# Cross-attention and bit-weight FFN on one core: more softmax tiles turned by DMA, their values last in TensorE's step

## The chip, the cores and the metric

One NeuronCore of a Trainium2 chip runs the whole program. The time is the device time of that core in microseconds; of the runs of a kernel the median is taken.

## The reference

The input is x (4, 1024, 1024), the context ctx (4, 1024, 1024), and the weights of a linear layer that are given as four sigmoid "bits" per weight. All is float32.

```python
x = x + attention(layernorm(x), ctx, ctx)       # 16 heads of 64, causal, softmax over keys, scale 1/8
weight = einsum('oin,n->oi', sigmoid(pweight) - sigmoid(nweight), exps * sigmoid(mask)) * scale
bias   = round(|clip(einsum('on,n->o', pbias - nbias, bexps), -1, 1)| * 15) / 15 * sign * biasscale
x = x + einsum('bsi,oi->bso', layernorm(x), weight) + bias
```

Keys and values are both the context as it stands; there are no projections.

## The kernel before

**Work.** The 4 x 1024 query rows are 32 tiles of 128 rows, t = 0..31, eight per batch; i = t % 8 is the place in the batch, and a tile sees i + 1 blocks of 128 keys. A tile is cut into jobs: four heads each for i = 0 and 1 (4 jobs), two for i = 2 and 3 (8 jobs), one for i = 4 to 7 (16 jobs, the "long tiles"). q is a job's place in its tile, n its number over the whole program (352 jobs), and a job has `blocks` = heads x (i + 1) blocks of probabilities, each 128x128. Products are made to near float32 accuracy by splitting an operand into a high and a low float16 part: scores take two matmuls, values three.

**A job's life.** PE (TensorE) makes the scores in PSUM (`slot`, two places, L397 to L421). DVE (VectorE) takes the row maxima (L642). ACT (ScalarE) makes the exponentials p in SBUF (`p32`, two places, L537) and their row sums. Then p must be turned, so that the keys lie on the partitions. In the usual way PE transposes the blocks into PSUM (`ptb`, two banks, L429), in chunks of at most four blocks; ACT writes the high parts into `pt` (L553), DVE the low parts (L648). Some jobs are "turned" by DMA instead (`j.d` is their count, L57): ACT scales and rounds p into the high part right after its exponentials (L546), DVE writes the low part beside it from SBUF (L656), both in `p16`, and the SP queue issues one DMA transpose of both parts into `ptd` (L320). PE then multiplies the turned probabilities by the values (L449, L450, L452) into `obank`, four heads to a group. When a group's last job is in, DVE's `output` divides by the row sums (L662, L667) and sets `obank` free, and POOL (GpSimd) adds the result to the row of x in `ring` (L870).

**The order.** Nothing is scheduled by a program; each engine's list is written out by hand as a loop over the jobs, and semaphores tie the engines. "Step j" of an engine is the turn of that loop for job j:

- PE: scores(j+2), values(j-2), transposes(j), then a share of the FFN's matmuls for tile t-3 (L468, 48 per tile).
- ACT: high parts of j (this first waits until values(j-2) are done, L550, also when j has none), exponentials(j+2) with the copy L546 if j+2 is turned, and at some steps the high part of a context, q or y tile.
- DVE: maxima(j+2), the low part L656 if j+1 is turned, output of the group that j-2 closed, low parts of j, then at some steps statistics for a layer norm (L674, L677) or a half of the FFN's result (L709).
- POOL: the add of a closed group (L870), at step 2 of a long tile the low part of y (L856), at 6 that of the context (L851), at 9 the bias (L864), at 11 the low part of q (L845); at 5 and at the end of a tile it normalises a row (L828).
- SP: the DMAs; in step s the transposition of job s + 1, loads of x and the context at step 9, the transposes of context, q and y (16 blocks each), the store of a result.

Of a long tile, jobs q = 3, 6, 9, 12, 15 are turned before, and of a tile of two heads (t > 3) jobs 3 and 6: 92 jobs. `p16` and `ptd` are the two halves of the tensor `pd`, which holds weights at the start.

## Time and profile before

| | |
|---|---|
| runs of the kernel before, median of 3 | 1187.38 us (1184.31 to 1188.52) |
| the profiled execution | 1185.72 us |
| its span, first to last instruction | 1183.9 us |
| TensorE clock granted, mean of the span | 0.990 |
| busy: PE / DVE / ACT / POOL | 1098.5 / 994.4 / 862.3 / 492.7 us |

The profile follows one execution. "Busy" is time in which an engine has an instruction under way; matmuls are pipelined and their ends modelled, so PE's share reads high. DVE and ACT start an instruction some 0.1 us before the one ahead has drained, so the durations of neighbours overlap. A timeline row gives start, duration, engine, line, operation and tile; in brackets stands the idle time of the engine ahead of it and what ended it.

### The profile page before, as it was taken

How to read it: one execution, taken by the hardware profiler on the slowest of the kernel's cores; microseconds unless marked ns; L12 is line 12 of the kernel's file. 1: busy time of each engine (PE TensorE's matmuls, PEld its weight loads, DVE VectorE, ACT ScalarE, POOL GpSimd, SP SyncE). 2: the span in 40 equal slices, each digit the busy share in tenths (PEclk: the TensorE clock that was granted, in tenths of full speed). 3: DMA queues.
4: the chain of work that ended last, by engine and by line, in shares of the span. 5: the costliest groups of instructions: out<-in, count | busy, mean ns of one | idle time of the engine just before them, and what ended most of it. 6: DMA issues, size and time to landing. Idle time of an engine off the chain costs nothing.

```text
span 1183.9 us, 32049 instructions
## 1 busy us (share of the span) xinstructions
PE 1098.5 (93%) x13092; PEld 808.7 (68%) x13092; DVE 994.4 (84%) x1552; ACT 862.3 (73%) x1770; POOL 492.7 (42%) x510
## 2 busy tenths in 40 slices
PE   3778888999999999999999999999999999999988
PEld 3666665666766777777776777777776676777753
DVE  5765688899988988998988888999988888998962
ACT  5887865777786777778776777777786777877740
POOL 3343534433334754344235654343335655331150
PEclk9999999999999999999999999999999999999999
DMA  8999936577659877775678887667768976654443
GB/s 308 301 295 337 299 80 120 134 146 122 151 121 186 189 180 131 162 160 112 132 121 203 194 173 148 139 140 130 137 125 205 185 171 131 137 117 86 89 90 71
DMA packets 382594, 191.13 MB, mean 161 GB/s; under 512 B 358128, under 2 KB 358128, under 8 KB 378352
## 3 DMA queue, kind: packets, MB, share of 16 engines
q1 hardware_dynamic: 381440, 189.05, 70.4%
q8 instruction: 104, 1.70, 0.6%
q14 instruction: 42, 0.34, 0.1%
q10 hardware_dynamic: 1008, 0.04, 0.1%
HBM read 67.15 MB, written 16.78 MB: 71 GB/s over the span
## 4 chain that ended last, share of the span: by engine, by line
PE 47%; DVE 18%; ACT 14%; DMA 7%; issue 7%; SPq 4%; POOL 3%; ACTq 0%; POOLq 0%; DVEq 0%
PE ffnb L468 15%; PE ptb L429 8%; PE slot L415 5%; PE slot L416 5%; DVE pd L656 4%; ACT p L537 4%; DVE mx L642 4%; DMA pd<-pd 4%; ACT pd L546 4%; PE obank L449 4%; ACT pt L553 4%; PE obank L452 3%; DVE stats L674 3%; PE obank L450 3%; DVE pt L648 3%
## 5 line engine op out<-in xcount | busy, mean ns | idle before, releaser
L537 ACT ACTIVATE p<-slot,mx 128x512 f32<-128x512 f32 (+7 forms) x512 | 377.4, 745 | 135.1 <-issue 71.2
L642 DVE TENSOR_REDUCE mx<-slot 128x1 f32<-128x640 f32 (+7 forms) x352 | 356.0, 1014 | 32.0 <-PE slot L419 31.3
L468 PE MATMUL ffnb<-wt,yt 128*128 128x512 f16 x1464 | 372.1, 380 | 1.1 <-DMA yt<-y 0.8
L648 DVE SCALAR_TENSOR_TENSOR pt<-ptb,pt 128x512 f16<-128x512 f32 (+1 forms) x504 | 281.6, 598 | 51.8 <-ACT pt L553 50.3
L553 ACT ACTIVATE pt<-ptb 128x512 f16<-128x512 f32 (+1 forms) x504 | 239.9, 526 | 106.0 <-PE ptb L429 104.8
L415 PE MATMUL slot<-kt,qt 128*128 128x128 f16 (+3 forms) x1056 | 267.2, 283 | 14.0 <-ACT p L537 5.9
L416 PE MATMUL slot<-kt,qs 128*128 128x128 f16 (+3 forms) x1056 | 267.2, 283 | 0.0
L870 POOL TENSOR_TENSOR ring<-ring,att 128x256 f32<-128x256 f32 x128 | 94.2, 736 | 394.0 <-DVE att L667 393.9
L429 PE MATMUL ptb<-id,p 128*128 128x128 f32 x1700 | 238.3, 279 | 10.9 <-DVE pt L648 10.8
L468 PEld LDWEIGHTS ffnb<-wt,yt 128*128 128x128 f16 x1464 | 137.2, 98 | 100.1 <-issue 2.2
L449 PE MATMUL obank<-v,pt 128*128 128x64 f16 x1700 | 176.9, 193 | 16.3 <-DVE att L667 12.1
L429 PEld LDWEIGHTS ptb<-id,p 128*128 128x128 f32 x1700 | 181.9, 141 | 13.9 <-issue 12.3
L449 PEld LDWEIGHTS obank<-v,pt 128*128 128x128 f16 x1700 | 153.5, 98 | 35.6 <-DVE att L667 20.1
L450 PE MATMUL obank<-v,pt 128*128 128x64 f16 x1700 | 176.7, 193 | 0.0
L452 PE MATMUL obank<-v,pt 128*128 128x64 f16 x1700 | 176.7, 193 | 0.0
L415 PEld LDWEIGHTS slot<-kt,qt 128*128 128x128 f16 x1056 | 103.4, 98 | 79.5 <-ACT p L537 11.7
L452 PEld LDWEIGHTS obank<-v,pt 128*128 128x128 f16 x1700 | 151.8, 98 | 0.0
L450 PEld LDWEIGHTS obank<-v,pt 128*128 128x128 f16 x1700 | 151.6, 98 | 0.1
L416 PEld LDWEIGHTS slot<-kt,qs 128*128 128x128 f16 x1056 | 103.6, 98 | 56.4
L656 DVE SCALAR_TENSOR_TENSOR pd<-p,pd 128x640 f16<-128x640 f32 (+3 forms) x92 | 111.8, 1215 | 13.5 <-ACT pd L546 10.5
L419 PE MATMUL slot<-maskb,idb 128*128 128x128 bf16 x512 | 110.3, 220 | 0.0
L537 ACT ACTIVATION_READ_ACCUMULATOR p<-slot,mx 128x1 f32 x512 | 106.4, 208 | 0.0
(92 smaller groups left out, 1528.7 us busy)
## 6 DMA issues: line engine op xcount, KB each, us to landing
ring<-in_x_dram SPq DMA_DIRECT2D x32, 512.0 KB, 4.5
cin<-in_ctx_dram SPq DMA_DIRECT2D x32, 512.0 KB, 4.9
out_dram<-ring SPq DMA_DIRECT2D x32, 512.0 KB, 3.3
qs<-qt SPq DMA_DIRECT2D x124, 128.0 KB, 2.9
v<-in_weights_dram SPq DMA_DIRECT2D x11, 1024.0 KB, 8.1
kt<-in_weights_dram SPq DMA_DIRECT2D x11, 1024.0 KB, 8.0
pd<-in_weights_dram SPq DMA_DIRECT2D x5, 1024.0 KB, 7.3
yt<-in_weights_dram SPq DMA_DIRECT2D x5, 1024.0 KB, 10.0
```

The lines of the kernel that those rows point to most:

```text
L415: pe.matmul(dst, qt[:, t % 2, h, :], keys, start=True, stop=False, skip_group_check=True)
L416: last = pe.matmul(dst, qs[:, h, :], keys, start=False, stop=end <= i, skip_group_check=True)
L429: last = pe.transpose(ptb[:, c % 2, at * P:(at + 1) * P], p32[:, j.par, k * P:(k + 1) * P], id32[:, :])
L449: pe.matmul(dst, turned[:, k, :], v[:, 0:D], start=blk == 0, stop=False, skip_group_check=True)
L450: pe.matmul(dst, turned[:, k, :], v[:, D:2 * D], start=False, stop=False, skip_group_check=True)
L452: last = pe.matmul(dst, turned[:, j.blocks + k, :], v[:, 0:D], start=False, stop=blk == j.i, skip_group_check=True)
L468: last = pe.matmul(dst, yt[:, k % 2, a * KT_N + kk, :], wt[:, c, kk, half * 512:half * 512 + 512], start=r == 0, stop=r == 3 * KT_N - 1)
L537: last = nc.scalar.activation(p32[:, j.par, hh * j.keys:(hh + 1) * j.keys], slot[:, j.par, base:base + j.keys], ACT.Exp, bias=mx[:, j.par, ...
L553: nc.scalar.activation(pt[:, j.par, blocks.start:blocks.stop, :], ptb[:, c % 2, 0:P * len(blocks)].rearrange("p (k c) -> p k c", c=P), ACT ...
L642: nc.vector.tensor_reduce(mx[:, j.par, 0:j.heads], src[:, 0:j.heads, 0:j.keys], AX_X, ALU.max, negate=True).then_inc(mx_ready, 1)
L648: nc.vector.scalar_tensor_tensor(pt[:, j.par, j.blocks + blocks.start:j.blocks + blocks.stop, :], ptb[:, c % 2, 0:P * len(blocks)].rearran ...
L656: nc.vector.scalar_tensor_tensor(p16[:, size:2 * size], p32[:, j.par, 0:size], P_SCALE, p16[:, 0:size], ALU.mult, ALU.subtract).then_inc(p ...
```

## The change

It changes which jobs are turned by DMA: in a long tile each odd q (8 of 16 instead of 5), in a tile of two heads q = 3, 5, 7 (3 of 8 instead of 2), 146 jobs in all. They have two places each for the split (`p16`) and for the turned form (`ptd`): `pd` grows to three parts, two for `p16`; the second place of `ptd` is `pt[:, 1]`, which the usual way used for odd jobs. The semaphore of the landing is doubled with them, and the waits follow the places. PE does the values of a turned job as the last thing of step j + 2, after the FFN's matmuls, no longer right after the scores; DVE's output of a group that a turned job closed goes from the middle of the step to its end. In a long tile every group is closed by a turned job.

```diff
--- before.py
+++ after.py
@@ -54,7 +54,7 @@
         self.blocks = blocks = self.heads * (self.i + 1)
 
 
-        self.d = turned if self.heads < 3 and t > 3 and q > 0 and q % 3 == 0 else None
+        self.d = turned if self.heads < 3 and t > 3 and q % 2 and q >= self.heads * 2 - 1 else None
         count = -(-blocks // 4) if self.d is None else 0
         size = -(-blocks // count) if count else 0
         self.chunks = [(chunk0 + c, range(size * c, min(size * c + size, blocks))) for c in range(count)]
@@ -70,6 +70,13 @@
         JOBS.append(Job(len(JOBS), _t, _q, sum(len(j.chunks) for j in JOBS), sum(j.d is not None for j in JOBS)))
 FIRST.append(len(JOBS))
 TURNED = [j for j in JOBS if j.d is not None]
+
+def used_before(j):
+
+    earlier = [k.n for k in JOBS[:j.n] if (k.d % 2 == j.d % 2 if k.d is not None else j.d % 2 and k.par)]
+    return earlier[-1] + 1 if earlier else 0
+
+
 LAST_OF_GROUP = [j.n for j in JOBS if j.closes_group]
 
 
@@ -187,7 +194,7 @@
         v16 = sb("v16", [P, V_PLACES, H, 2 * D], F16)
         kt16 = sb("kt16", [P, K_PLACES, H, P], F16)
         ring = sb("ring", [P, RING, DM], F32)
-        pd = sb("pd", [P, 2, 2 * 8 * P], F16)
+        pd = sb("pd", [P, 3, 2 * 8 * P], F16)
         cin = sb("cin", [P, DM], F32)
         norm32 = sb("norm32", [P, DM], F32)
         q16 = sb("q16", [P, H, 2 * D], F16)
@@ -215,8 +222,8 @@
         bvec = sb("bvec", [P, 8], F32)
 
 
-        p16 = pd[:, 0]
-        ptd = pd[:, 1].rearrange("p (k c) -> p k c", c=P)
+        p16 = [pd[:, 0], pd[:, 1]]
+        ptd = [pd[:, 2].rearrange("p (k c) -> p k c", c=P), pt[:, 1]]
 
 
         def chunk_place(places):
@@ -226,7 +233,7 @@
                  chunk_place(kt16[:, 7:9].rearrange("p a h c -> p (a h c)")),
                  chunk_place(kt16[:, 5:7].rearrange("p a h c -> p (a h c)")),
                  chunk_place(v16[:, 6:8].rearrange("p a h c -> p (a h c)")),
-                 chunk_place(pd[:, :, :].rearrange("p a c -> p (a c)")),
+                 chunk_place(pd[:, 0:2, :].rearrange("p a c -> p (a c)")),
                  chunk_place(yt[:, :, :, :].rearrange("p a k c -> p (a k c)"))]
         coef_diag = ring[:, 6, 0:NBITS * P].rearrange("p (n q) -> p n q", n=NBITS)
 
@@ -265,7 +272,8 @@
 
         s_done, mx_ready, p_done = sem("s_done"), sem("mx_ready"), sem("p_done")
         t_done, hi_done, lo_done, pv_done = sem("t_done"), sem("hi_done"), sem("lo_done"), sem("pv_done")
-        p16_hi, p16_lo, pt_in = sem("p16_hi"), sem("p16_lo"), sem("pt_in")
+        p16_hi, p16_lo = sem("p16_hi"), sem("p16_lo")
+        pt_in = [sem(f"pt_in{r}") for r in range(2)]
         osb_done = sem("osb_done")
         rinv_ready, x1_ready = sem("rinv_ready"), sem("x1_ready")
         q_stats, q_mv, q_rs, q_norm, q_hi, q_lo = (sem("q_" + n) for n in ("stats", "mv", "rs", "norm", "hi", "lo"))
@@ -315,9 +323,9 @@
 
             def turn_p(j):
                 sp.wait_ge(p16_lo, j.d + 1)
-                if j.d > 0:
-                    sp.wait_ge(pv_done, TURNED[j.d - 1].n + 1)
-                sp.dma_start_transpose(ptd[:, 0:2 * j.blocks], p16[:, 0:2 * P * j.blocks]).then_inc(pt_in, 16)
+                reached(sp, pv_done, used_before(j))
+                sp.dma_start_transpose(ptd[j.d % 2][:, 0:2 * j.blocks], p16[j.d % 2][:, 0:2 * P * j.blocks]
+                                       ).then_inc(pt_in[j.d % 2], 16)
 
             def swap_q(t, half):
                 heads = slice(H // 2 * half, H // 2 * (half + 1))
@@ -438,8 +446,8 @@
                 if j.d is None:
                     pe.wait_ge(lo_done, j.chunks[-1][0] + 1)
                 else:
-                    pe.wait_ge(pt_in, 16 * (j.d + 1))
-                turned = pt[:, j.par] if j.d is None else ptd
+                    pe.wait_ge(pt_in[j.d % 2], 16 * (j.d // 2 + 1))
+                turned = pt[:, j.par] if j.d is None else ptd[j.d % 2]
                 for hh in range(j.heads):
                     h = j.head0 + hh
                     for blk in range(j.i + 1):
@@ -510,7 +518,7 @@
             for j in JOBS:
                 if j.n + 2 < len(JOBS):
                     scores(JOBS[j.n + 2])
-                if j.n > 1:
+                if j.n > 1 and JOBS[j.n - 2].d is None:
                     values(JOBS[j.n - 2])
                 transpose_p(j)
                 if j.n < UNITS:
@@ -519,6 +527,8 @@
                     bias_part(j.n - BIAS_JOBS[0])
                 for k, m0, m1 in matmuls_at(j.t, j.q):
                     linear(k, m0, m1)
+                if j.n > 1 and JOBS[j.n - 2].d is not None:
+                    values(JOBS[j.n - 2])
             values(JOBS[-2])
             values(JOBS[-1])
             pe.wait_ge(p_done, len(JOBS))
@@ -541,9 +551,9 @@
                 last.then_inc(p_done, 1)
                 if j.d is not None:
                     act.wait_ge(p_done, j.n + 1)
-                    reached(act, pt_in, 16 * j.d)
+                    reached(act, pt_in[j.d % 2], 16 * (j.d // 2))
                     size = P * j.blocks
-                    nc.scalar.activation(p16[:, 0:size], p32[:, j.par, 0:size], ACT.Copy, scale=P_SCALE
+                    nc.scalar.activation(p16[j.d % 2][:, 0:size], p32[:, j.par, 0:size], ACT.Copy, scale=P_SCALE
                                          ).then_inc(p16_hi, 1)
 
             def high_parts(j):
@@ -653,8 +663,9 @@
             def low_part_unturned(j):
                 dve.wait_ge(p16_hi, j.d + 1)
                 size = P * j.blocks
-                nc.vector.scalar_tensor_tensor(p16[:, size:2 * size], p32[:, j.par, 0:size], P_SCALE,
-                                               p16[:, 0:size], ALU.mult, ALU.subtract).then_inc(p16_lo, 1)
+                split = p16[j.d % 2]
+                nc.vector.scalar_tensor_tensor(split[:, size:2 * size], p32[:, j.par, 0:size], P_SCALE,
+                                               split[:, 0:size], ALU.mult, ALU.subtract).then_inc(p16_lo, 1)
 
             def output(g):
                 dve.wait_ge(p_done, LAST_OF_GROUP[g] + 1)
@@ -777,8 +788,9 @@
                     maxima(JOBS[j.n + 2])
                 if j.n + 1 < len(JOBS) and JOBS[j.n + 1].d is not None:
                     low_part_unturned(JOBS[j.n + 1])
-                if j.n > 1 and JOBS[j.n - 2].closes_group:
-                    output(JOBS[j.n - 2].group)
+                ended = JOBS[j.n - 2] if j.n > 1 and JOBS[j.n - 2].closes_group else None
+                if ended is not None and ended.d is None:
+                    output(ended.group)
                 low_parts(j)
                 if j.n + 1 < UNITS:
                     first_difference(j.n + 1)
@@ -801,6 +813,8 @@
                             result(k, half)
                 for k in y_begun(t, s):
                     y_moments(k)
+                if ended is not None and ended.d is not None:
+                    output(ended.group)
             output(GROUPS * TILES - 1)
             spare = slot[:, 0, 0:512]
             for k in range(TAIL, TILES):
```

In the compiled order DVE's list shows what a turned job meets. The rows are of a tile of eight key blocks (i = 7); `mx<-slot` are maxima, `pd<-p,pd` the low part of a turned job, `pt<-ptb,pt` low parts of one that PE transposes. Before:

```order
L656 SCALAR_TENSOR_TENSOR pd<-p,pd 128x1024
L648 SCALAR_TENSOR_TENSOR pt<-ptb,pt 128x512 x2
L642 TENSOR_REDUCE mx<-slot 128x1
L674 BN_STATS stats<-ring 128x6 x2
L677 BN_AGGR mv<-stats 128x2
L642 TENSOR_REDUCE mx<-slot 128x1
L648 SCALAR_TENSOR_TENSOR pt<-ptb,pt 128x512 x2
L642 TENSOR_REDUCE mx<-slot 128x1
L656 SCALAR_TENSOR_TENSOR pd<-p,pd 128x1024
L662 RECIPROCAL rinv<-rowsum 128x4
L667 SCALAR_TENSOR_TENSOR att<-obank,rinv 128x256
```

And in the changed kernel, the same kind of tile:

```order
L678 SCALAR_TENSOR_TENSOR att<-obank,rinv 128x256
L652 TENSOR_REDUCE mx<-slot 128x1
L667 SCALAR_TENSOR_TENSOR pd<-p,pd 128x1024
L658 SCALAR_TENSOR_TENSOR pt<-ptb,pt 128x512 x2
L652 TENSOR_REDUCE mx<-slot 128x1
L685 BN_STATS stats<-ring 128x6 x2
L688 BN_AGGR mv<-stats 128x2
L652 TENSOR_REDUCE mx<-slot 128x1
L667 SCALAR_TENSOR_TENSOR pd<-p,pd 128x1024
L658 SCALAR_TENSOR_TENSOR pt<-ptb,pt 128x512 x2
L652 TENSOR_REDUCE mx<-slot 128x1
```

Between the maxima of a turned job and its low part stood two low parts `pt` and the next maxima; now the next maxima stand there alone, at some steps with an output or statistics. Of each two steps, one has the low parts of both kinds, the other none.

On PE, of a tile with five key blocks, `obank<-v,pd` are values of a turned job and `ffnb<-wt,yt` the FFN's matmuls. In the kernel before, the values stand right behind the scores:

```order
L415 MATMUL slot<-kt,qt 128x128
L416 MATMUL slot<-kt,qs 128x128
L419 MATMUL slot<-maskb,idb 128x128
L449 MATMUL obank<-v,pd 128x64
L450 MATMUL obank<-v,pd 128x64
L452 MATMUL obank<-v,pd 128x64
L449 MATMUL obank<-v,pd 128x64
```

In the changed kernel the FFN's matmuls come between:

```order
L424 MATMUL slot<-kt,qs 128x128
L427 MATMUL slot<-maskb,idb 128x128
L476 MATMUL ffnb<-wt,yt 128x512 x3
L457 MATMUL obank<-v,pd 128x64
L458 MATMUL obank<-v,pd 128x64
L460 MATMUL obank<-v,pd 128x64
L457 MATMUL obank<-v,pd 128x64
L458 MATMUL obank<-v,pd 128x64
```

## Rows read from the trace of the kernel before

**Rows 1.** The page, its first part: busy time of each engine.
```profile
PE 1098.5 (93%) x13092; PEld 808.7 (68%) x13092; DVE 994.4 (84%) x1552; ACT 862.3 (73%) x1770; POOL 492.7 (42%) x510
```
**Rows 2.** Windows on the four long tiles of the second batch; columns as the first line says.
```profile
core 0: us, PE busy (x) PEld busy (x) DVE busy (x) ACT busy (x) POOL busy (x), PEclk, DMA share, GB/s
444.60:483.60 39.00, 36.90 (x501) 27.39 (x497) 33.18 (x62) 27.45 (x63) 18.87 (x19) 1.00 0.73 146
...
567.40:614.30 46.90, 46.12 (x625) 34.23 (x624) 43.80 (x60) 37.43 (x63) 15.93 (x16) 1.00 0.73 135
sum 169.70, PE 163.73 PEld 122.21 DVE 153.46 ACT 129.89 POOL 66.84; mean PE 40.93 PEld 30.55 DVE 38.37 ACT 32.47 POOL 16.71
```
**Rows 3.** Timeline of DVE around a turned job, eight key blocks.
```profile
843.03 1.23 DVE L656 SCALAR_TENSOR_TENSOR pd<-p,pd 128x1024 f16<-128x1024 f32 x1 [0.25 <-ACT pd L546]
844.17 1.28 DVE L648 SCALAR_TENSOR_TENSOR pt<-ptb,pt 128x512 f16<-128x512 f32 x2
845.37 1.21 DVE L642 TENSOR_REDUCE mx<-slot 128x1 f32<-128x1024 f32 x1
846.50 1.27 DVE L674 BATCH_NORM_STATS2 stats<-ring 128x6 f32<-128x512 f32 x2
...
847.94 1.17 DVE L642 TENSOR_REDUCE mx<-slot 128x1 f32<-128x1024 f32 x1
```
**Rows 4.** Timeline of ACT in the same stretch.
```profile
840.70 1.12 ACT L537 ACTIVATE p<-slot,mx 128x1024 f32<-128x1024 f32 x1
...
841.94 1.06 ACT L546 ACTIVATE pd<-p 128x1024 f16<-128x1024 f32 x1
...
846.67 1.11 ACT L537 ACTIVATE p<-slot,mx 128x1024 f32<-128x1024 f32 x1 [1.60 <-issue]
```
**Rows 5.** Groups by line and shape: x count | busy us, mean ns | idle before.
```profile
L642 DVE TENSOR_REDUCE mx<-slot 128x1 f32<-128x1024 f32 x64 | 77.4, 1210 | 2.2 <-PE slot L419 1.9
L537 ACT ACTIVATE p<-slot,mx 128x1024 f32<-128x1024 f32 x64 | 71.5, 1117 | 30.5 <-issue 25.5 <-PE obank L452 3.6 <-DVE mx L642 1.2
L642 DVE TENSOR_REDUCE mx<-slot 128x1 f32<-128x640 f32 x64 | 51.4, 808 | 5.9 <-PE slot L419 5.9
L537 ACT ACTIVATE p<-slot,mx 128x640 f32<-128x640 f32 x64 | 51.0, 797 | 27.2 <-DVE mx L642 17.5 <-issue 7.3 <-PE obank L452 2.4
L546 ACT ACTIVATE pd<-p 128x640 f16<-128x640 f32 x20 | 14.7, 737 | 1.2 <-DMA pd<-pd 0.6
L648 DVE SCALAR_TENSOR_TENSOR pt<-ptb,pt 128x512 f16<-128x512 f32 x232 | 151.3, 683 | 28.3 <-ACT pt L553 27.6
L648 DVE SCALAR_TENSOR_TENSOR pt<-ptb,pt 128x384 f16<-128x384 f32 x228 | 119.3, 549 | 23.6 <-ACT pt L553 22.7
L648 DVE SCALAR_TENSOR_TENSOR pt<-ptb,pt 128x256 f16<-128x256 f32 x44 | 18.2, 413 | 0.0
```
**Rows 6.** The line L656 of DVE: duration ns shortest/median/longest, then the wait ahead of it.
```profile
L656 DVE SCALAR_TENSOR_TENSOR pd<-p,pd x92: 812/1092/2432, 194.9 to 1140.4; 128x768 f16<-128x768 f32 x26, 128x1024 f16<-128x1024 f32 x26, 128x640 f16<-128x640 f32 x20, 128x896 f16<-128x896 f32 x20
```
**Rows 7.** Timelines of DVE and POOL, six key blocks, where a group is closed.
```profile
773.46 0.94 DVE L642 TENSOR_REDUCE mx<-slot 128x1 f32<-128x768 f32 x1
...
778.82 2.14 DVE L656 SCALAR_TENSOR_TENSOR pd<-p,pd 128x768 f16<-128x768 f32 x1
...
775.02 0.73 POOL L870 TENSOR_TENSOR ring<-ring,att 128x256 f32<-128x256 f32 x1 [3.89 <-DVE att L667]
775.71 2.35 POOL L864 TENSOR_TENSOR ring<-ring,bias_row 128x1024 f32<-128x1024 f32 x1
778.02 2.13 POOL L845 TENSOR_TENSOR q<-norm,q 128x1024 f16<-128x1024 f32 x1
```
**Rows 8.** Timeline of PE's weight loads: the transposes of one job of six blocks.
```profile
921.54 0.64 PEld L429 LDWEIGHTS ptb<-id,p 128*128 128x128 f32 x6
```
**Rows 9.** SP's issue of the turned jobs' transposes (ns), and median us from issue to landing.
```profile
L320 SPq DMA_TRANSPOSE pd<-pd x92: 1274/1440/3463, 197.0 to 1141.7; - x92
...
pd<-pd SPq DMA_TRANSPOSE x92, 4.1
```

## The prediction

> **What bounds the kernel now.** I read the busy times first: PE 93% and DVE 84% of the span [rows 1]. Then windows, since such shares are means: in the four long tiles of a batch (169.7 us, and that four times in the 1184 of the span) PE is busy for 163.7, DVE for 153.5, ACT for 129.9 [rows 2]. With eight key blocks PE has work in 46.1 of 46.9 us and DVE in 43.8; with five, 36.9 and 33.2 of 39.0. So PE is the bound in the longest tiles, DVE stands 5 to 10% behind it, and whatever PE gives up, DVE soon takes over. The third view is the timeline around a turned job: ahead of its low part DVE has been idle for 0.25 us, until ACT's copy was done [rows 3]. DVE's filler (two low parts and one maxima) just about covers the way of a turned job through ACT. That is the place to watch, since the change takes the filler out.
>
> **PE.** There are 54 more turned jobs. Per batch the long tiles get three more each, of 5, 6, 7 and 8 blocks: 78 blocks, 312 in all. The two-head tiles with t > 3 get one more each, of 6 or 8 blocks, three times: 42. That makes 354 transposes fewer. Six take 0.64 us of weight loads [rows 8], 0.107 each, so PE sheds 37.9 us. Nothing else leaves PE; the values only move within a step.
>
> **ACT and DVE, by work alone.** With eight blocks an extra turned job takes two low parts of 0.68 from DVE [rows 5] and gives it one of 1.23 [rows 3]; with five it takes 0.55 + 0.41 and gives 0.81, the shortest of the line [rows 6]. DVE gains 0.13 to 0.15 a job, nothing that matters. DVE therefore still needs about 153 us of these tiles, where PE now needs 163.7 - 78 x 0.107 = 155.4.
>
> **The loop that the order makes.** In the changed order two steps hang together in a ring: maxima of turned job o, its exponentials (ACT), its copy (ACT), its low part (DVE), the low parts of job o - 1 (DVE, behind it in DVE's list), then the maxima of o + 2. Between the maxima of o and its low part DVE has only the maxima of o + 1. Eight blocks, link by link: maxima 1.21; 0.09 to the exponentials (846.58 to 846.67) [rows 3, 4], the longer gap of a job whose forerunner by two was turned, which now is every turned job; exponentials 1.12 [rows 5]; 0.12 to the copy, copy 1.06, 0.03 to DVE (843.00 to 843.03) [rows 3, 4]; low part 1.14 from start to start, low parts of o - 1 1.20 from start to start [rows 3]. Sum **5.97 us for two steps**, 47.8 for the tile, against 46.9 measured. Five blocks: 0.81 + 0.09 + 0.80 + 0.12 + 0.74 + 0.03 + 0.74 + 0.80 [rows 5, 6], neighbours on DVE overlapping by 0.08 (846.58 to 846.50) [rows 3], = 4.13, 33.0 for the tile, against 39.0. Six and seven lie evenly between, 4.74 and 5.36. The four tiles take 161.6 us by the ring. It is longer than PE's 155.4 and DVE's 153, so neither engine is the bound: their hand-over is.
>
> **What comes on top on DVE.** In the ring DVE is idle between the maxima of o + 1 and the low part of o. The way there is 2.42 us with eight blocks and 1.78 with five, the maxima fill 1.13 and 0.73: 1.29 and 1.05 idle. Outputs fit in. At step 3 stand the statistics of q, 1.44 from start to start of what follows (846.50 to 847.94) [rows 3], too long by 0.15 to 0.39. At step 15 half a result (512 columns from PSUM like a chunk of low parts, 0.60) and the statistics of y, 2.04, too long by 0.75 to 0.99. Over the four sizes: 4.6 us a batch.
>
> **What comes on top from POOL.** One low part of a turned job in the trace took 2.14 us, and it ended 0.81 us after POOL's low part of q (778.02 + 2.13 = 780.15, then 780.96) [rows 7]; the lone duration for six blocks lies between the 0.81 of five and the 1.23 of eight, near 0.95. It stood still for all but 0.15 us of the overlap. I take it that of DVE's work here only this line is stopped: it alone reads two tensors in SBUF, the others read PSUM or one tensor. Where do the new low parts meet POOL? The output of a group comes at the end of steps 1, 5, 9 and 13, right behind maxima. From the end of those maxima to POOL's add it is 0.62 us (774.40 to 775.02), the add lasts 0.69, and behind it stands at step 9 the bias, 2.35 [rows 7], at step 1 the low part of y, same shapes as that of q, 2.13. POOL is so busy until 3.66 and 3.44 us after the maxima; the low part of q = 11 and of q = 3 is due after 1.78 to 2.42. It is late by 1.24 to 1.88 and 1.02 to 1.66, less the 0.15: 1.09 to 1.73 and 0.87 to 1.51. Over four sizes 5.6 and 4.8, together **10.4 us a batch**. Before, job 3 had a step's low parts more ahead of it and job 11 wasn't turned; job 12 met the low part of q, and the measured 169.7 holds that already.
> The Trainium skill, page SBUF — State Buffer, section "SBUF: two separate sides", says that VectorE and GpSimd share a pair of ports by an exclusive lock: an op with two SBUF inputs against a GpSimd op that reads SBUF "fully blocks" for the whole instruction. Without the 0.15 us of grace each stall would be longer by that, 1.2 us a batch, 5 us in all; the row of 2.14 us speaks for the shorter figure, and the rule speaks for the stall as such and against this change.
>
> **Other edits.** The doubled places let the transposition of job o start without waiting for the values of the turned job before; before, the issue came after it anyway, so I cost that at nothing, bounds 0 and -2 us. Values last: with the ring as the bound PE idles some 0.5 us a pair of steps at eight blocks (46.1 - 24 x 0.107 = 43.5, an eighth is 5.44, against 5.97), which covers it; were PE late, the exponentials of o + 2 (they wait for values(o - 2), and the high parts stand behind them) and the next group's first values (behind DVE's output) would be next. SP has 54 more issues of 1.44 us [rows 9] with nothing urgent behind. DMA: a turned job lands 4.1 us after issue [rows 9]. Its values must be done before ACT begins the exponentials of the job four later: low parts, a whole ring, maxima and gap after its own low part, 0.80 + 4.13 + 0.90 = 5.8 us with five blocks, 1.20 + 5.97 + 1.30 = 8.5 with eight. That leaves 1.7 us for the values at five blocks, with DMA engines that are 73% busy already [rows 2]: the cover is thin only there. Cost 0, bounds 0 and +20 us. Two-head tiles: 42 transposes of the 354, 4.5 us; I take half, 2.2, with bounds 0 and 4.5, since DVE does the low parts of y, context and q there.
>
> **Sum.** By batch 161.6 + 4.6 + 10.4 = 176.6 against 169.7: +6.9. By size: five blocks 33.0 + 1.4 + 3.2 = 37.6 (39.0 before, so faster), eight blocks 47.8 + 0.9 + 2.0 = 50.7 (46.9 before, slower by 8%). Four batches: +27.6, less 2.2: +25.4. The profiled execution took 1185.7, so 1211; the median shown is 1.7 above it, and the three casts a tile on ACT, which I haven't priced, can only delay the exponentials: **1214 us**.
>
> **Rivals.**
> *PE's gain comes through.* If the copy comes early enough that DVE never waits for it, PE stays the bound: 1187 - 38 = **1149**. For it: PE's 98% of the longest tile. Against it: DVE already waits with two low parts more as filler [rows 3], and DVE's own work needs 153 of 155. It decides if the way from maxima to low part is under 1.2 us at eight blocks; the links add up to 2.42. Chance 0.10.
> *The ring holds, POOL slips by.* If POOL's work starts later than I place it, in the stretch of the next maxima, the 10.4 us go: 166.2 a batch, -3.5 x 4 - 2.2 = -16, **1171**. This is the other side by one mechanism, at steps 2 and 10, decided by whether POOL's work begins over 1.2 us later than in rows 7. Against it: the add waits for DVE's output alone. Chance 0.13.
> *The DMA becomes late.* 146 transposes in place of 92, with the engines at 73%. If landings stretch from 4.1 to over 6 us, five and six blocks pay about 1 us a job, 64 jobs: +20 to +30 on top, **1240**. Chance 0.09.
>
> **Chances.** My forecast has 0.68, with a range of its own of 1195 to 1232. A measurement tells about 0.3% from no change. Slower by more: 0.68 + 0.09 less a little for the low edge, 0.75; faster by more: 0.10 + 0.13 less a little, 0.20; within, 0.05. The range leaves out PE's gain (0.10) and the far end of the late DMA: 1165 to 1243.
>
> **What would show it.** The waits: DVE's low part of a turned job waits for ACT's copy at nearly each of the 146 (0.25 us where it shows before, 0.9 to 1.3 us now), some 60 to 120 us in all, the largest wait of DVE. The same line's longest durations fall on q = 3 and q = 11, near 2.5 us and more at five blocks. PE's busy time falls by some 38 us while the span grows. Windows: tiles of five blocks shorter, of eight blocks near 50 us. I am wrong if DVE's idle time ahead of that line stays under 30 us, if the eight-block tiles take 46 us or less, or if PE waits long for the landing.

## The result, and the profile after

The changed kernel takes **1246.28 us** (median of 4 runs, 1242.72 to 1248.6); the kernel before took 1187.95 in the same series (4 runs, 1184.31 to 1188.95). The ratio is 1.0499, 95% interval 1.0474 to 1.0525: slower by 58 us, where 27 were forecast. It lies 14 us above the forecast's own range (1195 to 1232) and 3 us above the wide one (1165 to 1243). The direction was right, the size was not.

The page of the changed kernel, busy time of each engine, against [rows 1]:

```profile
PE 1086.3 (88%) x12738; PEld 775.4 (62%) x12738; DVE 1024.0 (83%) x1498; ACT 860.2 (69%) x1716; POOL 529.0 (43%) x510
```

PE's share fell from 93% to 88%, DVE's hardly moved: no engine is the bound. Weight loads fell by 33 us of the 38 forecast, PE's modelled busy time by 12 only; part of the gap is the clock (last section). Waits of the changed kernel (engine, line, what it waited for: us in total, times, longest), and of the kernel before, a choice of rows:

```profile
PEld obank L457 <- DVE att L678: 94.5, 72, 4.0
...
DVE pd L667 <- ACT pd L556: 76.9, 103, 1.9
PE obank L457 <- DVE att L678: 76.5, 70, 3.9
ACT p L547 <- PE obank L460: 70.2, 52, 3.1
...
ACT pt L563 <- PE obank L460: 16.3, 6, 3.7
```

```profile
PEld obank L449 <- DVE att L667: 20.9, 32, 1.5
...
ACT p L537 <- PE obank L452: 13.2, 14, 1.3
PE obank L449 <- DVE att L667: 12.5, 28, 1.2
...
DVE pd L656 <- ACT pd L546: 10.5, 32, 0.9
```

Two kinds of wait have grown. The one that the prediction named, DVE's low part behind ACT's copy, is 76.9 us in 103 times (of 146 turned jobs, where "nearly each" was forecast; in the pairs that begin with jobs 1 and 5 DVE's own list fills the gap). The other it named only to put it at nothing: PE's values wait for DVE's output (76.5 against 12.5), and ACT for PE's values, partly at its high parts (16.3 us in 6 times, up to 3.7 at once; before, no such row).

Where the time lies: windows of the long tiles of the second batch (columns as in [rows 2]), then of the short tiles behind them, after and before.

```profile
454.80:497.20 42.40, 37.59 (x485) 26.41 (x485) 35.82 (x57) 28.19 (x61) 19.84 (x18) 0.96 0.87 178
497.20:538.40 41.20, 37.03 (x484) 26.58 (x483) 36.74 (x57) 30.48 (x59) 17.61 (x16) 1.00 0.86 166
538.40:583.90 45.50, 40.70 (x540) 29.02 (x539) 40.81 (x57) 33.84 (x59) 18.36 (x16) 1.00 0.79 161
583.90:633.30 49.40, 44.19 (x600) 31.34 (x600) 44.49 (x57) 37.16 (x59) 19.02 (x16) 1.00 0.84 157
```
```profile
633.30:650.60 17.30, 16.04 (x191) 11.76 (x190) 10.82 (x19) 10.51 (x36) 2.93 (x5) 0.90 0.85 179
650.60:671.90 21.30, 18.75 (x172) 12.71 (x173) 20.64 (x34) 15.27 (x48) 13.65 (x16) 1.00 0.83 173
671.90:700.80 28.90, 28.90 (x355) 21.26 (x352) 27.60 (x45) 20.08 (x50) 20.13 (x21) 1.00 0.96 172
700.80:734.50 33.70, 29.05 (x332) 21.35 (x329) 27.80 (x37) 21.50 (x47) 17.45 (x17) 0.95 0.72 147
```
```profile
614.30:629.90 15.60, 14.59 (x198) 10.73 (x199) 12.13 (x22) 11.55 (x41) 5.63 (x9) 1.00 0.84 162
629.90:648.40 18.50, 18.50 (x170) 12.47 (x167) 17.45 (x29) 13.41 (x41) 9.82 (x11) 1.00 0.83 194
648.40:678.00 29.60, 29.60 (x362) 21.98 (x359) 27.73 (x47) 21.25 (x53) 19.58 (x21) 1.00 0.82 192
678.00:706.00 28.00, 28.00 (x347) 21.60 (x343) 24.56 (x39) 21.56 (x48) 16.82 (x17) 1.00 0.81 165
```

The four long tiles take 178.5 us, against 169.7 before and 176.6 forecast. The tiles of i = 0, 1 and 3 (the first, second and fourth row of the second fence), where the change was costed at nothing or as a small gain, grew by 1.7, 2.8 and 5.7 us. The same by tile, as the mean over batches 2 to 4 (us; i = 7 without the last), for all kernels measured. A tile runs from the moment at which PE has the scores of its first job to the same moment of the next tile:

| i | before | after | a | b | e | f | c | d | lock | h | k | l |
|---|---|---|---|---|---|---|---|---|---|---|---|---|
| 0 | 15.7 | 17.2 | 17.2 | 17.3 | 15.7 | 16.8 | 16.8 | 17.4 | 17.1 | 15.8 | 15.8 | 15.8 |
| 1 | 18.6 | 21.0 | 18.7 | 18.6 | 21.7 | 20.9 | 20.6 | 21.4 | 19.8 | 18.6 | 18.8 | 18.6 |
| 2 | 29.5 | 28.8 | 28.8 | 28.9 | 29.5 | 30.2 | 28.8 | 28.8 | 28.8 | 28.9 | 28.8 | 28.8 |
| 3 | 28.0 | 33.7 | 27.1 | 29.0 | 29.7 | 29.6 | 33.0 | 33.6 | 33.1 | 27.1 | 27.1 | 27.1 |
| 4 | 39.2 | 42.6 | 40.6 | 42.6 | 44.3 | 40.2 | 42.8 | 42.5 | 38.1 | 39.5 | 40.7 | 39.7 |
| 5 | 40.0 | 41.2 | 41.8 | 41.2 | 44.3 | 41.3 | 40.3 | 41.1 | 38.8 | 40.2 | 41.0 | 40.8 |
| 6 | 44.0 | 45.5 | 45.5 | 45.5 | 49.2 | 45.3 | 43.5 | 45.1 | 43.3 | 43.7 | 45.7 | 46.0 |
| 7 | 47.4 | 49.4 | 49.5 | 49.5 | 51.9 | 49.5 | 47.3 | 49.4 | 47.3 | 47.1 | 50.9 | 49.9 |

A batch lost 17 us: 8 in the long tiles, 9 in the short ones. The letters are those of the experiments below (lock is i_lock).

**The ring.** DVE in the tile of eight blocks (start, duration, line, form; in brackets the idle time ahead and what ended it):

```profile
607.77 1.21 DVE L652 TENSOR_REDUCE mx<-slot 128x1 f32<-128x1024 f32 x1
...
609.10 0.42 DVE L678 SCALAR_TENSOR_TENSOR att<-obank,rinv 128x256 f32<-128x256 f32 x1
609.44 1.21 DVE L652 TENSOR_REDUCE mx<-slot 128x1 f32<-128x1024 f32 x1
611.39 1.23 DVE L667 SCALAR_TENSOR_TENSOR pd<-p,pd 128x1024 f16<-128x1024 f32 x1 [0.74 <-ACT pd L556]
612.53 1.28 DVE L658 SCALAR_TENSOR_TENSOR pt<-ptb,pt 128x512 f16<-128x512 f32 x2
613.73 1.21 DVE L652 TENSOR_REDUCE mx<-slot 128x1 f32<-128x1024 f32 x1
...
619.70 1.21 DVE L652 TENSOR_REDUCE mx<-slot 128x1 f32<-128x1024 f32 x1
...
623.32 2.33 DVE L667 SCALAR_TENSOR_TENSOR pd<-p,pd 128x1024 f16<-128x1024 f32 x1 [0.74 <-ACT pd L556]
...
626.78 2.34 DVE L652 TENSOR_REDUCE mx<-slot 128x1 f32<-128x1024 f32 x2
```

From the maxima of a turned job to those of the next it is 5.96 us (607.77 to 613.73), then 5.97, with the output inside the idle time: the ring as added up. With five to eight blocks the pairs without an extra (those that begin with jobs 7 and 13) take 4.12, 4.74, 5.35 and 5.97 us in nearly every tile, against 4.13, 4.74, 5.36 and 5.97 forecast. The last pair, of job 11, takes 7.08: its low part lasted 2.33. POOL at that time:

```profile
622.21 2.36 POOL L878 TENSOR_TENSOR ring<-ring,bias_row 128x1024 f32<-128x1024 f32 x1
624.53 3.12 POOL L859 TENSOR_TENSOR q<-norm,q 128x1024 f16<-128x1024 f32 x1
```

The bias ends at 624.57, the low part 1.08 later: it stood still for 1.10 us, forecast 1.09.

**What was not foreseen.** The seam between the long tiles and the next batch. At step 1 of the tile i = 0 the values of q = 15 of the tile before are due. PE, ACT and DVE there, in the changed kernel:

```profile
646.01 2.75 PE L476 MATMUL ffnb<-wt,yt 128*128 128x512 f16 x12
648.60 0.19 PE L457 MATMUL obank<-v,pt 128*128 128x64 f16 x1
...
653.15 0.20 PE L457 MATMUL obank<-v,pt 128*128 128x64 f16 x1 [2.59 <-DVE att L678]
649.50 0.60 ACT L563 ACTIVATE pt<-ptb 128x512 f16<-128x512 f32 x1 [3.74 <-PE obank L460]
650.13 0.69 DVE L658 SCALAR_TENSOR_TENSOR pt<-ptb,pt 128x512 f16<-128x512 f32 x1 [3.67 <-ACT pt L563]
652.67 0.42 DVE L678 SCALAR_TENSOR_TENSOR att<-obank,rinv 128x256 f32<-128x256 f32 x1
```

This step's own job is not turned, so ACT has high parts to write, and they wait for the values of j - 2. The transposes and twelve FFN matmuls now stand ahead of those values: ACT waits 3.74 us, DVE 3.67 behind it. DVE's output then comes last in its step, after y and a result, and PE, which must have it before the next group's first values, stands for 2.59 us. The six waits of ACT's high parts for values are all of this kind: three fall in tiles with i = 0, three in tiles with i = 3. Within a long tile there are none, since each step that ends with late values belongs to a turned job, which has no high parts. PE does wait for DVE's output inside the long tiles too (51.6 of the 76.5 us), but the late order isn't what makes the time there: with the old one (a_early, below) the tiles of six to eight blocks take 41.8, 45.5 and 49.5 us, no less than here.

### The profile page after: what moved, and what is told of

It reads as the page before. It is cut to its first block, busy times and chain, and to the rows that moved or that the text cites. A ratio compares the mean times of both kernels' runs of the same rounds, so it can differ in the third digit from the quotient of the medians.

```text
span 1240.9 us, 31340 instructions
## 1 busy us (share of the span) xinstructions
PE 1086.3 (88%) x12738; PEld 775.4 (62%) x12738; DVE 1024.0 (83%) x1498; ACT 860.2 (69%) x1716; POOL 529.0 (43%) x510
## 4 chain that ended last, share of the span: by engine, by line
PE 51%; DVE 17%; ACT 4%; issue 4%; DMA 4%; POOL 1%; SPq 1%; DVEq 0%; POOLq 0%; ACTq 0%
PE ffnb L476 19%; PE ptb L437 8%; PE slot L423 5%; PE slot L424 5%; DVE pd L667 5%; PE obank L457 4%; DVE pt L658 4%; DMA pt<-pd 4%; DVE mx L652 4%; PE obank L460 3%; PE obank L458 3%; ACT pd L556 2%; DVE att L678 2%; DVE stats L685 1%; PE slot L476 1%
## 5 line engine op out<-in xcount | busy, mean ns | idle before, releaser
L476 PE MATMUL ffnb<-wt,yt 128*128 128x512 f16 x1464 | 378.1, 385 | 1.7 <-DVE ring L720 0.9
L884 POOL TENSOR_TENSOR ring<-ring,att 128x256 f32<-128x256 f32 x128 | 100.2, 783 | 451.1 <-DVE att L678 451.1
L423 PE MATMUL slot<-kt,qt 128*128 128x128 f16 (+3 forms) x1056 | 269.0, 284 | 24.2 <-ACT p L547 20.6
L457 PE MATMUL obank<-v,pt 128*128 128x64 f16 x1828 | 193.0, 195 | 96.2 <-DVE att L678 76.5
L667 DVE SCALAR_TENSOR_TENSOR pd<-p,pd 128x768 f16<-128x768 f32 (+3 forms) x146 | 203.2, 1392 | 77.3 <-ACT pd L556 76.9
L563 ACT ACTIVATE pt<-ptb 128x512 f16<-128x512 f32 (+2 forms) x396 | 189.2, 526 | 95.9 <-PE ptb L437 79.2
L457 PEld LDWEIGHTS obank<-v,pt 128*128 128x128 f16 x1828 | 164.5, 98 | 138.5 <-DVE att L678 94.5
L658 DVE SCALAR_TENSOR_TENSOR pt<-ptb,pt 128x512 f16<-128x512 f32 (+2 forms) x396 | 222.7, 600 | 28.9 <-ACT pt L563 28.2
L437 PE MATMUL ptb<-id,p 128*128 128x128 f32 x1346 | 195.7, 286 | 1.1 <-DVE pt L658 1.1
L460 PE MATMUL obank<-v,pt 128*128 128x64 f16 x1828 | 192.3, 194 | 0.0
L458 PE MATMUL obank<-v,pt 128*128 128x64 f16 x1828 | 192.2, 194 | 0.0
L458 PEld LDWEIGHTS obank<-v,pt 128*128 128x128 f16 x1828 | 164.4, 99 | 6.8
L460 PEld LDWEIGHTS obank<-v,pt 128*128 128x128 f16 x1828 | 164.6, 99 | 0.0
L437 PEld LDWEIGHTS ptb<-id,p 128*128 128x128 f32 x1346 | 150.3, 145 | 1.6 <-issue 1.2
L556 ACT ACTIVATE pd<-p 128x768 f16<-128x768 f32 (+3 forms) x146 | 132.0, 904 | 4.6
```

What stands on the lines that cost most here:

```text
L423: pe.matmul(dst, qt[:, t % 2, h, :], keys, start=True, stop=False, skip_group_check=True)
L437: last = pe.transpose(ptb[:, c % 2, at * P:(at + 1) * P], p32[:, j.par, k * P:(k + 1) * P], id32[:, :])
L457: pe.matmul(dst, turned[:, k, :], v[:, 0:D], start=blk == 0, stop=False, skip_group_check=True)
L458: pe.matmul(dst, turned[:, k, :], v[:, D:2 * D], start=False, stop=False, skip_group_check=True)
L460: last = pe.matmul(dst, turned[:, j.blocks + k, :], v[:, 0:D], start=False, stop=blk == j.i, skip_group_check=True)
L476: last = pe.matmul(dst, yt[:, k % 2, a * KT_N + kk, :], wt[:, c, kk, half * 512:half * 512 + 512], start=r == 0, stop=r == 3 * KT_N - 1)
```

## The experiments

Ten kernels. a, b, e and f ask about the order, c about the ring, d and i about POOL, h, k and l which jobs to turn. Edits are shown against the changed kernel where nothing else is said.

**a_early: the change without its order.** Values and output of a turned job stand where the kernel before has them.

```diff
-                if j.n > 1 and JOBS[j.n - 2].d is None:
+                if j.n > 1:
                     values(JOBS[j.n - 2])
...
-                if j.n > 1 and JOBS[j.n - 2].d is not None:
-                    values(JOBS[j.n - 2])
...
-                if ended is not None and ended.d is None:
+                if ended is not None:
...
-                if ended is not None and ended.d is not None:
-                    output(ended.group)
```

> The changed kernel with one part undone: values of a turned job again right behind the scores, the output of its group again in the middle of DVE's step; the choice of jobs and the two places stay. Theory A (what my sum left out is the new order in steps whose own job is not turned: there the high parts on ACT wait for values that now come after transposes and the FFN's matmuls, and PE's next group waits for an output that stands behind statistics and results on DVE): the two-head tiles with eight blocks fall from 33.7 us back to about 28, the four-head tiles from 17 and 20-21 to under 16 and 19, the first long tile from 42.5 to about 39; the other long tiles stay at 41, 45.5 and 49. In all some 25 to 30 us less, 1217 to 1222. Rival B (the 54 more transposes crowd SP's queue and the DMA engines, and that makes the short tiles long): the short tiles stay where they are and PE waits more for landings, since values are wanted earlier: 1246 or more.

Measured: 1215.13 us (1213.21 to 1217.19), ratio to before 1.0237 (1.02 to 1.0273). The late order costs 31 us, more than half of the loss, and what is left is within 2 us of the forecast for the whole. By tile, i = 1, 3 and 4 give back 2.3, 6.6 and 2.0 us. Two points of the expectation didn't come: i = 0 stayed at 17.2 us, and i = 4 fell to 40.6, not to 39.

**b_both: late only where the step's own job is turned too.**

```diff
-                if j.n > 1 and JOBS[j.n - 2].d is None:
+                if j.n > 1 and (JOBS[j.n - 2].d is None or j.d is None):
                     values(JOBS[j.n - 2])
```

and the same condition at the three other places.

> The changed kernel with values last and the output at the end only in steps whose own job is turned too (that is inside long tiles and at steps 5 and 7 of two-head tiles), the old order in all other steps. Theory A: as much as undoing the order altogether, 1217 to 1222, apart from what steps 5 and 7 of the two-head tiles keep. Rival B: no change, within 5 us of 1246.

Measured: 1222.76 (1219.89 to 1227.86), 1.0305 (1.0262 to 1.0349). Most of the 31 us are the seams: 23 come back. Step 1 of the tiles i = 0 and i = 3 are such steps. The rest lies at i = 3 (29.0 against 27.1) and i = 4 (42.6 against 40.6); at step 1 of i = 4 the own job is turned, but DVE's output comes last all the same, behind a result and statistics. ACT's waits at the exponentials for PE's values stay in b_both (64.3 us) and so cost little.

**e_late: the kernel before with the late order alone.** Its 92 turned jobs and single places stay. The edit, against the kernel before:

```diff
-                if j.n > 1:
+                if j.n > 1 and JOBS[j.n - 2].d is None:
                     values(JOBS[j.n - 2])
...
+                if j.n > 1 and JOBS[j.n - 2].d is not None:
+                    values(JOBS[j.n - 2])
```

and DVE's output in the same way.

> The kernel before with one part of the change alone: its own 92 jobs, one place each, but values of a turned job last in PE's step and DVE's output of a group that it closed at the step's end. In this choice of jobs nearly every such step has a job of its own that PE transposes. Theory A (ACT's high parts wait for values that now stand behind transposes and FFN matmuls of the same step, and everything after them waits with them): each of the 92 late steps pays about 1 us, the values' delay of a job's transposes plus three FFN matmuls (0.53 + 0.64 at five blocks, 0.86 + 0.64 at eight) less the slack of some 0.5: 60 to 120 us more, 1245 to 1305, and ACT's wait for PE's values becomes its largest. Rival (the place of the values costs nothing by itself, what undoing it brought was the DMA's or SP's): within 10 us of 1187.

Measured: 1270.56 (1266.99 to 1273.31), 1.071 (1.069 to 1.073). With every third job turned, each late step belongs to a job that PE transposes, and has high parts waiting: the loss is 84 us, in the long tiles too (i = 6 49.2 against 44.0). Its waits show the mechanism by itself:

```profile
PEld obank L449 <- DVE att L669: 81.6, 59, 2.5
ACT pt L555 <- PE obank L452: 76.1, 71, 3.4
```

71 waits of ACT's high parts for values, none in the kernel before and 6 in the changed one: the same order is dear or nearly free, according to whose step it stands in.

**f_long: turned jobs in long tiles only,** the order late.

```diff
-        self.d = turned if self.heads < 3 and t > 3 and q % 2 and q >= self.heads * 2 - 1 else None
+        self.d = turned if self.heads < 2 and t > 3 and q % 2 and q >= self.heads * 2 - 1 else None
```

> The changed kernel with turned jobs in the long tiles only, none in the two-head tiles. Theory A: the eight-block two-head tile falls from 33.7 to 28 or 29 us and the four-head tiles that follow a long one keep their 17, since the last two turned jobs of a long tile still come late there; the first long tile falls from 42.5 to 39 or 40, the rest stays: some 25 us less, near 1221. A rival by which the long tiles' own DMA load makes the short ones slow would leave them at 33.

Measured: 1225.53 (1223.95 to 1229.32), 1.0338 (1.0317 to 1.036). The tile i = 1 keeps its 2.3 us though no job near it is turned but the q = 15 of the batch before: the seam of the rows above. i = 3 falls from 33.7 to 29.6, i = 4 from 42.6 to 40.2.

**c_short: the ring shortened.** ACT's copy is cut to 128 columns from tile 8 on (the high part beyond is left from an earlier job, and the low part takes the difference).

```diff
                     size = P * j.blocks
+                    size = size if j.t < 8 else P
```

> The changed kernel with ACT's copy of a turned job cut to its first 128 columns from the second batch on (tiles 8 to 31); the rest of the high part is left as it stands, so the low parts and values are those of other numbers. All waits stay. Theory R (the ring maxima, exponentials, copy, low part, low parts sets the pace of long tiles): the copy gives back 0.45 us a pair at five blocks and 0.75 at eight, up to PE's own pace of 5.44 a pair at eight: some 0.5 us x 8 pairs x 12 long tiles = 48 us less, near 1200. Rival P (PE or the DMA sets the pace and DVE's wait for the copy is slack): under 10 us.

Measured: 1227.53 (1222.92 to 1229.76), 1.0333 (1.0284 to 1.0381), 19 us less, not 48. The long tiles take 4.8 us a batch less, none of it with five blocks. DVE's wait for the copy fell from 76.9 to

```profile
DVE pd L668 <- ACT pd L557: 32.7, 52, 1.3
```

The cut shortens the copy of an eight-block job from 1.06 to 0.31 us, by 0.75, and where nothing else stands in a pair all of it arrives. In the tiles of eight blocks the pairs that begin with jobs 7 and 13 fall from 5.97 to 5.22 (610.33 to 615.55), and that of job 15 takes 5.22 too, where a_early has 5.97:

```profile
610.33 1.22 DVE L653 TENSOR_REDUCE mx<-slot 128x1 f32<-128x1024 f32 x1
...
615.55 1.22 DVE L653 TENSOR_REDUCE mx<-slot 128x1 f32<-128x1024 f32 x1
```

The other pairs hardly move, and the trace has a reason for each. In those of jobs 1 and 5 (6.58 and 5.98 us with either copy) DVE works through statistics or a result without a gap. In those of jobs 3 and 11 (6.87 and 7.08) the low part ends when POOL's operation does: it starts earlier and stands still longer (2.84 us instead of 2.34 at job 11). That of job 9 gains 0.24: in it DVE now waits for PE's scores (0.45 us). With five blocks job 13 gains 0.43 us and job 9 loses 0.75, because its low part now meets POOL (1.8 us instead of 0.9). So with eight blocks the ring alone sets the pace of three pairs in eight; my expectation gave the gain to all eight.

**d_bias: POOL's bias cut to one column** (the bias is left out of the rest).

```diff
-                nc.gpsimd.tensor_tensor(row, row, bias_row[:, :], ALU.add).then_inc(bias_added, 1)
+                nc.gpsimd.tensor_tensor(row[:, 0:1], row[:, 0:1], bias_row[:, 0:1], ALU.add).then_inc(bias_added, 1)
```

> The changed kernel with POOL's bias add cut to one column of 1024, so the bias is left out of all others; all waits stay. Theory L (DVE's low part of job 11 stands still while POOL adds the bias, and the ring passes that on): 1.1 us a long tile at eight blocks to 1.7 at five, 16 tiles, 22 us less, near 1224, and the low part of job 11 takes its lone length, 0.82 to 1.23. Rival (the stall falls into slack): under 5 us, while the low part of job 11 is as short.

Measured: 1239.78 (1237.99 to 1243.68), 1.0449 (1.0408 to 1.0489). The time alone doesn't tell the theories apart. POOL's list closed up, and the low part of q took the place of the bias:

```profile
809.41 0.20 POOL L878 TENSOR_TENSOR ring<-ring,bias_row 128x1 f32<-128x1 f32 x1
809.55 2.14 POOL L859 TENSOR_TENSOR q<-norm,q 128x1024 f16<-128x1024 f32 x1
```

DVE's low part of job 11 still took 2.2 to 2.5 us in the first three batches. The last two tiles of the program do tell: no low part of q follows there, job 11's low part took 1.09 and 1.23 us, and its pair 5.35 and 5.97, where the changed kernel has 6.68 and 7.09 in the same tiles. So the stall is POOL's, and the ring passes all of it on.

**i_lock: the three long POOL operations cut together** (bias as above; the low parts of q and y are written for one head and one block, the rest is left out).

```diff
-                nc.gpsimd.tensor_tensor(y16[:, 1, :, :], norm32[:, :].rearrange("p (k c) -> p k c", c=P),
-                                        y16[:, 0, :, :], ALU.subtract).then_inc(y_lo, 1)
+                nc.gpsimd.tensor_tensor(y16[:, 1, 0:1, :], norm32[:, 0:P].rearrange("p (k c) -> p k c", c=P),
+                                        y16[:, 0, 0:1, :], ALU.subtract).then_inc(y_lo, 1)
```

> The changed kernel with three of POOL's adds cut to a stub: the bias to one column, the low part of q to one head, the low part of y to one block; what is cut is left out of the result. The bias alone didn't tell, since the low part of q moved up into its place. Theory L: DVE's low part of jobs 3 and 11 takes its lone length (0.82 to 1.23, not 1.74 to 2.58), and the ring passes it on: 1.1 to 1.8 us at job 11 and 0.8 to 1.6 at job 3, 9.7 us a batch, 39 in all, near 1207; the tile of eight blocks 49.4 to 47.4, that of five blocks 42.5 to about 39.5. Rival (slack): under 10 us.

Measured: 1199.36 (1195.57 to 1201.92), 1.0109 (1.0089 to 1.0129), 47 us less than the changed kernel. The line L667 (count, shortest/median/longest ns) has no long ones of that kind left at jobs 3 and 11:

```profile
L667 DVE SCALAR_TENSOR_TENSOR pd<-p,pd x146: 815/1082/2042, 189.3 to 1153.5; 128x768 f16<-128x768 f32 x41, 128x1024 f16<-128x1024 f32 x41, 128x640 f16<-128x640 f32 x32, 128x896 f16<-128x896 f32 x32
```

there they take 0.82 to 1.23 us, and the pair of job 11 with eight blocks 5.96. The long tiles give back 11.2 us a batch, against 10.4 forecast. The pairs say where: those of job 11 give back 1.76, 1.54, 1.33 and 1.12 us with five to eight blocks, those of job 3 1.05, 0.80, 0.86 and 0.90. That is 9.4 of the 11.2, near the 9.7 expected. Nearly all of the rest is the first pair of the five-block tile (7.67 to 6.15); POOL's results also come earlier, and that part this run can't tell from the stalls.

**h_best: what the parts suggest.** The order of the kernel before, its choice in the long tiles (q = 3, 6, 9, 12, 15), but jobs 3, 5, 7 in two-head tiles; only job 5 uses the second place. Of the edit, the lines that choose jobs and places:

```diff
-        self.d = turned if self.heads < 3 and t > 3 and q % 2 and q >= self.heads * 2 - 1 else None
+        self.d = turned if self.heads < 3 and t > 3 and (q >= 3 and q % 2 if self.heads == 2 else q > 0 and q % 3 == 0) else None
+        self.place = 1 if self.heads == 2 and q == 5 else 0
```

> A version for use: the kernel before with its order and its choice in the long tiles (every third job), and of the change only the two-head tiles' jobs 3, 5 and 7, job 5 with the second place. Undoing the order showed these tiles at 27.1 and 28.8 us where the kernel before has 28.0 and 29.5, while the long tiles lose. Theory: 1.6 us less a batch in three batches, 5 us, 1181 to 1183 against 1187; the long tiles as before. Rival (the gain of the two-head tiles is given back at the seam to the first long tile, where its third turned job is still under way): no difference.

Measured: **1179.55 us** (1177.45 to 1183.07, 6 runs) against 1186.37 for the kernel before (11 runs): 0.9948 (0.993 to 0.9966). It is faster than both, by 0.5% against the kernel before, with an interval that leaves out 1. The tiles i = 2 and 3 take 28.9 and 27.1 us, against 29.5 and 28.0: 1.6 us a batch, 4.8 in the three batches that have such jobs. In the profiled executions h_best is 8 us shorter; most of the other 3 lie in the first three tiles and ahead of them, where no job is turned in either kernel, and why isn't known.

**k_shift5 and l_shift4: other jobs of the long tile.** On h_best, five or four turned jobs, away from POOL's low part of q.

```diff
-        self.d = turned if self.heads < 3 and t > 3 and (q >= 3 and q % 2 if self.heads == 2 else q > 0 and q % 3 == 0) else None
+        self.d = turned if self.heads < 3 and t > 3 and (q >= 3 and q % 2 if self.heads == 2 else q % 3 == 1) else None
```

(l_shift4: `q > 1 and q % 3 == 1`.)

> This is h_best (the order of the kernel before; in two-head tiles jobs 3, 5, 7 turned) with the five turned jobs of a long tile moved from q = 3, 6, 9, 12, 15 to q = 1, 4, 7, 10, 13. In h_best DVE's low part of q = 12 meets POOL's low part of q, and stalls 1.6 / 1.2 / 0.7 / 0.3 us with 5 / 6 / 7 / 8 key blocks; at the new places no low part of a turned job should lie beside a long operation of POOL, except near the start of a tile. Theory 'POOL's lock is worth what it stalls': 3.8 us a batch are freed, all of it at five and six blocks, where PE isn't the bound; over four batches up to 15 us, and with half of it lost to PE 1168 to 1176 us. Rival 'it comes back': job 1's low part and transposition meet the normalising on POOL and the queue of transposes at the start of a tile, and the time is 1178 to 1188 us.

> As k_shift5, without job 1: four turned jobs in a long tile, q = 4, 7, 10, 13. PE gets back 5 to 8 transposes a long tile, 0.107 us each, 11 us in all if PE is the bound throughout. Theory 'POOL's lock': if k_shift5 loses by its job 1, this one gains against it; the lock freed (up to 15 us) less PE's 11 us gives 1172 to 1182 us. Rival 'the fifth turned job is worth its 11 us and the lock is hidden': 1186 to 1192 us.

Measured: k 1211.22 (1210.04 to 1212.54), 1.0212 (1.0184 to 1.024); l 1202.04 (1199.99 to 1203.43), 1.0136 (1.011 to 1.0161). k missed both expectations by 23 us, l by 10. The premise failed too: the turned jobs didn't get away from POOL. At step 6 of a long tile POOL writes the low part of the context, and with seven and eight blocks the low part of job 7 meets it. In k_shift5:

```profile
607.55 2.82 DVE L668 SCALAR_TENSOR_TENSOR pd<-p,pd 128x1024 f16<-128x1024 f32 x1 [0.25 <-ACT pd L557]
607.15 2.13 POOL L864 TENSOR_TENSOR v<-cin,v 128x1024 f16<-128x1024 f32 x1
```

It took 2.97 and 2.82 us in three of the four batches, where 1.09 and 1.23 are its lone lengths. With what is left at five and six blocks, such a batch has 3.9 us of stalls or a little more, against 3.8 for job 12 in h_best: nothing was freed, so the two runs don't test whether freeing it pays. The loss lies in the long tiles, most with eight blocks (50.9 and 49.9 against 47.1). Where a group begins, PE waits for DVE's output of the group before, and the transposes of the step stand behind: 31.7 us in k_shift5, 13.2 in h_best, but 9.2 in l_shift4. ACT's exponentials wait for PE's values for 47.4 and 43.3 us in the two, against 7.3 in h_best. Which of these reach the end, and so what the 32 and 22 us are made of, wasn't tried.

## Why the prediction was right and wrong

**The loop that the order makes: right.** The four pair times came out within 0.02 us of the sum of links. DVE's wait for the copy, 60 to 120 us forecast as its largest, was 76.9. That the ring is the bound holds for pairs without an extra: with a copy shorter by 0.75 us those with eight blocks fell by 0.75 (c_short). In the others DVE's own list, POOL or PE's scores are as long.

**What comes on top from POOL: right.** Low parts of job 11 took 2.58, 2.40, 2.42 and 2.34 us for five to eight blocks, those of job 3 2.38, 1.74, 1.94 and 2.12; without POOL 0.82 to 1.23. Summed stalls: 5.6 us a batch for job 11, to the tenth as forecast, and 4.1 for job 3, where 4.8 were. The rule of the Trainium skill (page SBUF — State Buffer, section "SBUF: two separate sides"), that of two such operations the one that comes second "fully blocks", agrees but for the 0.15 us: 2.33 us ended 1.08 after the bias, when 1.23 would be a full restart.

**The step that failed: "Values last", under Other edits,** costed at nothing because the ring leaves PE idle. The cover argued for was PE's, in the middle of a long tile. I named who waits for the values ("the high parts stand behind them") and for the output ("the next group's first values"), and then didn't walk the list of steps in which values are late and high parts exist: step 1 of the tiles i = 0 and i = 3, behind a tile with turned jobs. Nor did I look at what else DVE has in a step whose output moves to its end. There nothing covers it. Measured price: 31 us (a_early), 23 of them where the step's own job isn't turned (b_both). That is the 32 us between forecast and result: 1214 was in effect the forecast of a_early, 1215.13. That these two agree to 1 us is in part luck. Without the late order five blocks took 3.0 us more than forecast, seven and eight 0.8 and 1.2 less, and the tile i = 0, put at nothing, 1.5 more a batch.

**What comes on top on DVE: half the size at one place, nearly right at the other.** Statistics of q: 1.1 us a batch forecast; the pairs of job 5 show 0.25, 0.17, 0.10 and 0.01 above the ring. Half a result and statistics of y: 0.75 to 0.99 a tile forecast; they show in the first pair of the next tile, which is 0.77, 0.70 and 0.61 above the ring with six to eight blocks.

**The long tiles as a whole:** 178.7 us a batch (mean) against 176.6, and 177.4 without the late order. The split by size was off. Eight blocks took 49.4 where 50.7 were forecast. Five took 42.6 where 37.6 were: its first pair is 7.5 to 7.8 us, where the ring alone gives 4.13 and a_early, which has the old order, 5.52. The tile also begins with the last low part of a two-head job, eight blocks wide, which stands still for POOL (1.89 us at 456.77); the sum had no term for this seam. So "tiles of five blocks shorter" was wrong.

**Two-head tiles, -2.2 in all: too small.** By h_best they give 1.6 us in each of three batches, 4.8 us, twice the term and just above its bound of 4.5. In the changed kernel the late order turned the gain of i = 3 into +5.7.

**PE's busy time** was to fall by 38 us and fell by 12; its weight loads, from which the 38 were worked out, fell by 33.

**The rivals.** PE's gain coming through (1149): fell, the ring stood. POOL slipping by (1171): fell, by the lengths of jobs 3 and 11; but i_lock, 47 us faster, shows that it named the largest single price. The late DMA (1240): its time is nearest, its mechanism isn't there; PE's weight loads waited 17.5 us in 16 times for a landing in the second place and 3.9 in the first, against 8.4 before. (With the old order landings are wanted earlier: in a_early PE waits for them 26.3 us, 10.1 of it with five blocks.)

**The tile i = 0.** In every kernel with eight turned jobs in the long tiles it takes 16.8 to 17.4 us instead of 15.7, with either order. In a_early 0.9 of the 1.5 us is a matter of where tiles are cut: PE has the first scores 1.08 us before DVE's maxima of the same job, where it was 0.18 before, so this time is taken from the tile ahead. Another 0.5 is the last link of the ring: the low part of q = 15, which falls into this tile, waits 1.27 us for ACT's copy instead of 0.79.

## What to carry to other kernels

A step moved to the end of an engine's list must be priced at each kind of step where it occurs, the seams between tiles above all: find who waits for it there, and what that engine has queued behind the wait. A ring across engines can be added up from neighbouring rows to 0.02 us, but before taking a link out ask at each step what else stands there: here only three pairs in eight were the ring's alone. Before moving work away from a collision, list what it meets at the new place. Try the parts of a change alone: here one of three (two-head tiles, the old order) came with a gain of 0.5%, and the two others hid it.

## What the runs showed of the hardware

**The clock drops behind short waits.** In the kernel before PE's granted clock was full from 123.6 to 1147.6 us. The changed kernel has stretches at half. Windows around a PE wait in tile 12 (columns as in [rows 2]):

```profile
460.00:463.20 3.20, 1.04 (x23) 0.74 (x19) 3.13 (x8) 1.62 (x3) 0.00 (x0) 1.00 1.06 184
...
464.10:467.50 3.40, 3.40 (x16) 2.03 (x15) 1.44 (x4) 2.05 (x5) 2.58 (x4) 0.51 1.38 128
467.50:472.00 4.50, 4.50 (x66) 3.28 (x65) 3.48 (x5) 3.57 (x8) 2.50 (x2) 0.99 1.01 276
```

PE was busy for 1.04 of 3.20 us at the full clock (2.4 GHz) and without a gap for the next 0.90, then ran 3.40 us at half (1.2 GHz), 16 instructions in it, and then went back. Score matmuls of 384 columns followed each other by 0.32 us there (466.25 to 466.57), and by 0.16 elsewhere. Over the span the granted clock is 0.977 against 0.990: by my estimate 1240.9 x 0.023 - 1183.9 x 0.010 = 17 us of full clock more were withheld. So such a wait costs PE its own length and something on top; what of it reaches the end wasn't measured.

**The stall works both ways.** POOL's low part of q at 624.53 took 3.12 us instead of 2.13 [rows 7]: it began while DVE's low part, released by the end of the bias, was still under way until 625.65. Taking one POOL operation out moved the next into its place (d_bias), except in the last two tiles, where none follows; elsewhere only all three together freed DVE. In the changed kernel 46 low parts took over 0.15 us more than their lone length; each stood still for the overlap with POOL's operation less 0.13 to 0.15 us.
